# Pool stage of a four-layer graph network: matmul operands swapped, running maxima turned back, landing waits on GpSimd

## The reference, cut to what matters

```
def _graph_pool(out, adj):
    neg = jnp.finfo(out.dtype).min
    masked = jnp.where(adj_blk[:, :, None] != 0, out[None, :, :], neg)
    return jnp.max(masked, axis=1)          # for each block of rows
h = input @ weight
out = jnp.maximum(adj @ h + bias, 0.0)
return _graph_pool(out, adj)
```

## Time and profile before

| | us |
|---|---|
| median of three runs | 1762.82 (1762.29 to 1764.53) |
| profiled execution, own time | 1762.45 |
| its span, first to last instruction | 1760.7 |
| busy in the span: PE / DVE / ACT / POOL | 1564.3 / 1276.0 / 700.5 / 575.6 |
| mean granted TensorE clock | 0.965 of full |
| reduces of chunks (L1659), 256 | 172.8 |
| gathers of listed rows (L1302), 160 | 162.9 |
| selecting matmuls (L641), 3072 | 222.0 |

### The profile page before, as it was taken

The page is one execution under the profiler, slowest core; times in us unless marked ns, Lnnn a source line. Parts: engine busy times, 40 slices in busy tenths (PEclk is TensorE's granted clock), DMA queues, the critical chain, the costliest instruction groups (busy, mean ns, idle before and its releaser), DMA issues.

```text
span 1760.7 us, 37056 instructions
## 1 busy us (share of the span) xinstructions
PE 1564.3 (89%) x11433; PEld 1028.2 (58%) x11433; DVE 1276.0 (72%) x3508; ACT 700.5 (40%) x1113; POOL 575.6 (33%) x816
## 2 busy tenths in 40 slices
PE   3699999968888888999979999699999999889993
PEld 3467767647777777566646666578544444345552
DVE  5389999988999999455557666242599999944443
ACT  2334444425555555033332223466455555610000
POOL 2423233337777777011110001233000000047765
PEclk9999999988999999999999999899999999989997
DMA  4467777743433333222213223144100000024441
GB/s 156 174 250 262 289 271 288 286 151 90 122 113 101 113 100 116 82 96 95 93 34 125 83 88 114 55 132 125 37 1 6 6 12 6 6 91 154 152 140 48
DMA packets 97578, 205.11 MB, mean 116 GB/s; under 512 B 10912, under 2 KB 61728, under 8 KB 89328
## 3 DMA queue, kind: packets, MB, share of 16 engines
q1 hardware_dynamic: 73008, 172.58, 28.5%
q0 software_dynamic: 11840, 25.52, 5.2%
q10 hardware_dynamic: 12672, 6.29, 1.2%
HBM read 178.13 MB, written 26.21 MB: 116 GB/s over the span
## 4 chain that ended last, share of the span: by engine, by line
PE 45%; DVE 23%; issue 16%; POOL 9%; DMA 3%; ACT 2%; DVEq 1%; POOLq 1%; SPq 1%; ACTq 0%
PE bank L687 17%; PE bank L556 7%; PE bank L755 6%; DVE partsA L2063 6%; POOL gath L1385 5%; PE bank L822 4%; DVE gath L1659 3%; PE bank L641 3%; DVE cand L1526 2%; PE bank L561 2%; PE bank L541 2%; DMA gath<-last_features,idx_now 2%; PE bank L521 2%; POOL gath L1302 1%; PE bank L511 1%
## 5 line engine op out<-in xcount | busy, mean ns | idle before, releaser
L687 PE MATMUL bank<-partsB,panel 128*128 128x387 bf16 (+1 forms) x2048 | 354.5, 334 | 25.9 <-DVE agg L1460 12.1
L687 PEld LDWEIGHTS bank<-partsB,panel 128*128 128x128 fp8e4 x2048 | 202.7, 99 | 173.3 <-issue 27.1
L822 PE MATMUL bank<-wide,partsA 128*128 128x512 f32 x512 | 263.2, 596 | 6.3 <-ACT rows L1104 4.9
L641 PE MATMUL bank<-partsB,first 128*128 128x128 bf16 x3072 | 222.0, 221 | 35.6 <-DVE gath L1659 21.2
L1526 DVE MAX8 cand<-bank 128x8 f32<-128x128 f32 x1024 | 217.1, 279 | 42.1 <-POOL found L1213 21.7
L641 PEld LDWEIGHTS bank<-partsB,first 128*128 128x128 fp8e4 x3072 | 194.3, 98 | 80.7 <-issue 62.4
L556 PE MATMUL bank<-partsA,panel 128*128 128x387 bf16 x1024 | 218.1, 336 | 23.6 <-DVE cand L1526 14.3
L889 ACT ACTIVATE panel<-bank 128x1024 fp8e4<-128x1024 bf16 x128 | 130.7, 1023 | 175.9 <-PE bank L541 175.9
L1302 POOL DMA_INDIRECT gath<-pool_features,idx_now x160 | 162.9, 1018 | 55.3 <-issue 46.7
L1104 ACT COPY rows<-bank 128x512 f32<-128x512 f32 x256 | 133.3, 615 | 116.3 <-DVE partsA L2079 87.6
L1659 DVE TENSOR_REDUCE gath<-bank 128x128 f32<-128x512 f32 x256 | 172.8, 681 | 7.5 <-PE bank L641 7.1
(11 more groups left out here) (274 smaller groups left out, 2173.6 us busy)
## 6 DMA issues: line engine op xcount, KB each, us to landing
rows<-in_adj SPq DMA_DIRECT2D x64, 1024.0 KB, 7.2
panel<-adjT_panels SPq DMA_DIRECT2D x128, 512.0 KB
adjT_panels<-panel SPq DMA_DIRECT2D x32, 512.0 KB, 3.0
panel<-adjT_panels SPq DMA_DIRECT2D x64, 256.0 KB, 2.9
gath<-pool_features,idx_now POOLq DMA_INDIRECT x160
overflow_maxima<-wide POOLq DMA_DIRECT2D x1, 2048.0 KB, 19.1
pool_features<-gsc ACTq DMA_DIRECT2D x8, 256.0 KB, 2.3
rows<-overflow_maxima SPq DMA_DIRECT2D x8, 256.0 KB
```

Source lines behind the costliest of these rows:

```text
L641: i = pe.matmul(first_bank(n, peeled)[:, b * P:(b + 1) * P], first[:, q % 2, j, :], pparts[:, j, k * FE:k * FE + F], start=(k == 0), stop= ...
L687: i = pe.matmul(bank[q][:, 0:3 * w], panel[:, q, j, :], of_block if w < FE else parts_of[u][:, j, :], start=(j == 0), stop=(j == NT - 1))
L822: pe.matmul(o[:, :], zs[:, q % 2, :], zT[:, c * 512:(c + 1) * 512], start=True, stop=False)
```

## The change

TensorE. The operands of the selecting product are swapped: a 128 x 128 part of a block's features is stationary, and the selection codes of that block for *all four tiles* of the group (512 columns) stream past. So a step is now one block j of 32, with three matmuls of 512 columns, and its result has features as partitions and the group's 512 rows as columns. The triangular product is taken per block for four tiles (`tri_block`), from the panel laid out in pieces of four blocks (`piece`), six blocks ahead (`AHEAD`), through two banks. The selections lie in a ring of 16 slots.

VectorE. The maximum over blocks is now a running one of 128 x 512 in SBUF: blocks 0 and 1 are copied into two accumulators, blocks 2 to 31 are maxima of a bank with one of the accumulators in turn, and a last maximum joins the two. In the next group PE turns the result back by four transposes (`turn_firsts`), and `pool_floor` takes it from PSUM in a step of its own. The trees lose their first, widest step: only the five gathered rows remain, in three steps.

GpSimd. There are four slots for gathered rows and for indices, one for each tile of a group. `PAUSE` and `after_chunk` are gone. GpSimd waits till all five gathers of tile 0 have landed before those of tile 1, till tile 1's have landed before the overflow gathers, and till tile 2's have landed before those of tile 3. The scatter moves from the end of the group to behind tile 2's gathers.

SyncE loads eight pieces of 256 KB a group instead of four panels. ScalarE's copies for the next layer (`side_of`, `part0`) move into the group after, and the helper products use banks 6 and 7 of their own.

```diff
+        main = [gath[:, 0, 0:MAIN, :], gath[:, 1, 0:MAIN, :],
+                gath[:, 1, MAIN + FIRSTS + 1:2 * MAIN + FIRSTS + 1, :],
+                gath[:, 1, 2 * MAIN + FIRSTS + 1:3 * MAIN + FIRSTS + 1, :]]
+        running = gath[:, 0, MAIN:MAIN + FIRSTS, :].rearrange("p (a q) f -> p a (q f)", a=2)
-        tri_bank = [bank[2], bank[3], bank[6], bank[7]]
+        tri_bank = [bank[2], bank[3]]
...
             with sp.Fori(1, NG) as g:
-                for q in range(G):
-                    sp.wait_ge(s_tri, 8 * (g * G + q - G + 1))
-                    load_panel(g, q)
+                for c in range(NG):
+                    sp.wait_ge(s_tri, NT * (g - 1) + BPB * (c + 1))
+                    load_piece(g, c)
                 load_overflow(g - 1)
...
+            def tri_block(g, j):
+                if j % BPB == 0:
+                    pe.wait_ge(s_piece[j // BPB], 16 * (g + 1))
+                pe.wait_ge(s_first, NT * g + j + 1)
+                pe.matmul(tri_bank[j % 2][:, :], tri[:, :], piece[:, j // BPB, :, ts(j % BPB, P)],
                           start=True, stop=True).then_inc(s_tri, 1)
...
-                        for k in range(3):
-                            i = pe.matmul(first_bank(n, peeled)[:, b * P:(b + 1) * P], first[:, q % 2, j, :],
-                                          pparts[:, j, k * FE:k * FE + F], start=(k == 0), stop=(k == 2))
+            def select(g, j):
+                pe.wait_ge(s_first, NT * g + j + 3)
+                pe.wait_ge(s_fp_used, NT * g + j + 1)
+                for k in range(3):
+                    i = pe.matmul(pool_bank[j % 4][:, :], pparts[:, j, k * FE:k * FE + F], first_slot[:, j % SLOTS, :],
+                                  start=(k == 0), stop=(k == 2))
+                i.then_inc(s_fp, 1)
+            def turn_firsts(g):
+                pe.wait_ge(s_firsts_all, g + 1)
+                pe.wait_ge(s_side, g + 1)
+                for q in range(G):
+                    i = pe.transpose(psT[:, q * P:(q + 1) * P], firsts_all[:, q * P:(q + 1) * P], ident[:, :])
+                i.then_inc(s_turned, 1)
...
+            def rows_landed(g, q):
+                pool.wait_ge(s_gath[q], 16 * MAIN * (g + 1))
             def gathers(g, q):
                 t = g * G + q
                 pool.wait_ge(s_idx, t + 1)
                 pool.wait_ge(s_gath_used, t + 1)
+                if q in (1, 3):
+                    rows_landed(g, q - 1)
                 for k in range(MAIN):
-                    if k == PAUSE:
-                        after_chunk(t if q == 2 else t - 1, 1 if q == 2 else 6)
-                    pool.indirect_dma_start(gath[:, q % 2, k, :], None, feat_dram,
-                                            bass.IndirectOffsetOnAxis(idx_now[:, q % 2, k:k + 1], axis=0)
-                                            ).then_inc(s_gath[q % 2], 16)
+                    pool.indirect_dma_start(main[q][:, k, :], None, feat_dram,
+                                            bass.IndirectOffsetOnAxis(idx_now[:, q, k:k + 1], axis=0)
+                                            ).then_inc(s_gath[q], 16)
...
                     gathers(g, q)
                     if q == 1:
+                        rows_landed(g, q)
                         overflow_gathers(g)
-                store_overflow(g)
+                    if q == 2:
+                        store_overflow(g)
...
-                dve.tensor_reduce(gath[:, q % 2, MAIN + c, :],
-                                  first_bank(q * (NT // BPB) + c, peeled).rearrange("p (b f) -> p f b", b=BPB),
-                                  axis=AX, op=ALU.max).then_inc(s_fp_used, 1)
+            def take_block(g, j, first_group=False):
+                n = NT * g + j
+                if j < 2:
+                    if j == 0 and not first_group:
+                        dve.wait_ge(s_firsts_all, g)
+                    dve.wait_ge(s_fp, n + 1)
+                    dve.tensor_copy(running[:, j, :], pool_bank[j][:, :]).then_inc(s_fp_used, 1)
+                else:
+                    dve.wait_ge(s_fp_used, n + 3)
+                    dve.wait_ge(s_fp, n + 1)
+                    dve.tensor_tensor(running[:, j % 2, :], running[:, j % 2, :], pool_bank[j % 4][:, :], ALU.max
+                                      ).then_inc(s_fp_used, 1)
+                if j == NT - 1:
+                    dve.wait_ge(s_fp_used, n + 5)
+                    dve.tensor_tensor(firsts_all[:, :], running[:, 0, :], running[:, 1, :], ALU.max
+                                      ).then_inc(s_firsts_all, 1)
...
+                    dve.wait_ge(s_gath[q], 16 * MAIN * (g + 1))
+                    dve.tensor_tensor(slot[:, 0:2, :], slot[:, 0:2, :], slot[:, 2:4, :], ALU.max).then_inc(s_tree, 1)
...
+                for j in range(NT):
+                    take_block(g, j, peeled)
+                    if not (peeled or second):
+                        if j == 2:
+                            remainder(g - 2)
+                        if j == 25:
+                            part2(g - 2)
+                    if not peeled:
+                        if 3 <= j < 6:
+                            tree(before, G - 1, j - 3, (g, G - 1))
+                        if 6 <= j < 9:
+                            pool_floor(before, j - 6)
...
+                    for q, j0 in ((0, 11), (1, 17), (2, 26)):
+                        if j0 <= j < j0 + 3:
+                            tree(g, q, j - j0, None if last else (g + 1, q))
+                    if 21 <= j < 25:
+                        overflow_maxima(g, j - 21)
```

More of the change, by code:

```diff
@@ L36 @@
 MAIN = 5
-PAUSE = 3
+AHEAD = 6
+SLOTS = 16
 OVER = LIST - MAIN
@@ L603, in _ @@
                       ).then_inc(s_missing, 1)
+            for j in range(2, AHEAD):
+                tri_block(0, j)
             pe.wait_ge(s_flag, 1)
-            tri_chunk(0, 0, 2)
-            tri_chunk(0, 0, 3)
             pparts = parts_of[1]
[L610 to L626, removed]
@@ L663, in pool_turn @@
             def pool_turn(g, first_group, last):
[L664 to L675, removed]
+                for j in range(NT):
+                    if first_group:
+                        if j == 8:
+                            overflow_records()
+                    else:
+                        if j == 5:
+                            turn_firsts(g - 1)
+                        if j == 25:
+                            aux_transposes(1, g - 1)
+                        if j == 28:
+                            aux_products(1, g - 1)
+                    select(g, j)
+                    if j + AHEAD < NT:
+                        tri_block(g, j + AHEAD)
+                    elif not last:
+                        tri_block(g + 1, j + AHEAD - NT)
             pe.wait_ge(s_parts, 2 * NG)
@@ L912, in _, with first_block @@
             act.activation(DSTD[:, :], DEG[:, :], ACT.Sqrt).then_inc(s_sstd, 1)
[L914 to L919, removed]
-                                   tri_bank[c % 4][:, :], ACT.Relu, saturate=False).then_inc(s_first, 1)
+            def first_block(g, j, fresh=False):
+                act.wait_ge(s_tri, NT * g + j + 1)
+                if not (fresh and j < SLOTS):
+                    act.wait_ge(s_fp, NT * g + j - SLOTS + 1)
+                act.sem_inc(waited["act"], 1)
+                act.activation(first_slot[:, j % SLOTS, :], tri_bank[j % 2][:, :], ACT.Relu, saturate=False
+                               ).then_inc(s_first, 1)
             def after(u, s, g, more=None):
@@ L1757, in turn @@
                 before = 0 if second else g - 1
-                def at(q, c):
-                    take_firsts(g, q, c, peeled and q < 2, peeled)
-                at(0, 0)
-                if not (peeled or second):
-                    remainder(g - 2)
-                for c in range(1, 5):
-                    at(0, c)
-                    if not peeled:
-                        tree(before, G - 1, c - 1, (g, 1))
-                at(0, 5)
-                for c in range(6, 8):
-                    at(0, c)
-                    if not peeled:
-                        pool_floor(before, c - 6)
@@ L1774, in turn @@
-                if peeled:
-                    overflow_indices()
-                at(1, 0)
-                if not peeled:
-                    pool_post(before, 0)
-                for c in range(1, 5):
-                    at(1, c)
-                    tree(g, 0, c - 1, (g, 2))
-                if not (peeled or second):
-                    part2(g - 2)
-                for c in range(5, 8):
-                    at(1, c)
-                    if not peeled:
-                        pool_post(before, c - 4)
```

203 lines of the change are left out of this document (82 added, 121 removed).

## The result

The changed kernel takes 1787.05 us (median of four runs, 1786.95 to 1790.42) against 1763.09 for the kernel before on the same chip (four runs, 1762.29 to 1764.53): ratio 1.014 [1.0122, 1.0157]. The forecast was 1787.5. The profiled execution took 1786.95, 24.5 more than the 1762.45 of before.

What follows compares the result with a forecast made beforehand. GpSimd's gather issue, together with VectorE, was taken as the bound. Intervals 275.3, copies 7.0, slow gathers 9.6 and waits 36.0 made 327.9 us; with a shorter tail and 2 us for collisions, 1787.5, own range 1775 to 1798.

Steps and rivals of the forecast that it cites:

- the point on which all turned: GpSimd, 401 to 705 us: issues without a pause, about 5 us of 301 are waits; bounds the stage together with VectorE.
- slow gathers: GpSimd gathers held past 0.952 us by VectorE operations with two SBUF operands: 14.8 us before, 9.6 after.
- copies: GpSimd's one staging copy of overflow indices a group: 8 x 0.88, 7.0 us in the stage, before and after.
- landing waits: GpSimd, ahead of tile 1, overflow and tile 3 gathers: +2.05, +1.70, +0.75 us a group, 36.0 in all.
- 2 us for collisions: Added to the sum for gather landings that collide with the panel's 256 KB pieces: 2 us.
- The tail: From the last gather's start to the last group's normalised rows: 11.2 us instead of 14.9.
- TensorE and VectorE: Block of 2048 columns 0.875 us on TensorE, before 0.91; VectorE from 35.5 us busy a group to about 32.
- GpSimd does not bind: Rival for the gather stage: landing waits fall into idle time, groups run at 33.5 us, total 1729; chance 0.07.
- Waits at their lower bound: Rival on GpSimd's landing waits: 2.7 us a group, 21.6 in all, no holds, total 1764; chance 0.10 for 1764 to 1774.
- The dear case: Rival on GpSimd's gathers: block maxima hold them too (20 us), landings average 3.1 (16 us), total 1813; chance 0.13 above 1798.
- The Trainium skill's fit: Rival on gather landings: a 64 KB transfer takes 2.15 us, waits 7 us cheaper in all, total 1780; no chance given.

Runs made afterwards that it cites:

- experiments 1 to 5: Changed kernel with no landing waits (1747.71 us) or one of three (1765.23, 1762.60, 1756.06); kernel before with all three added, 1803.83 us.
- experiment 1: Changed kernel with its three landing waits taken out of GpSimd's list: 1747.71 us, ratio 0.9907; repeated, 1748.94 us, 0.9938.
- experiments 2 to 4: Changed kernel with only one landing wait kept: the first 1765.23 us, the second 1762.60, the third 1756.06.
- experiment 8: Changed kernel without landing waits, copy of the overflow indices moved ahead of tile 1's first gather: 1753.70 us, ratio 0.995.

## Why the prediction was right, point by point

**The bound.** That an engine with 74% busy share is the bound was the point on which all turned, and experiments 1 to 5 show it: taking waits away or adding them, in either order, moves the time by about what they add to GpSimd's stream. The stream of the changed kernel closes as that of before did. From the first gather's start (397.78) to the last's (731.23) are 220 intervals: 220 x 1.257 = 276.5; slow gathers 159.0 + 51.5 + 8.1 - 210.4 = 8.2; copies 2.7 + 6.5 - 8 x 0.30 = 6.8; landing waits 29.8 - 16 x 0.30 = 25.0 for first and third, 17.0 for the second. Together 333.5, measured 333.45.

**The terms.** Landing waits: 42.0, forecast 36.0, the one term that was clearly mis-sized. Per group the first and third took 3.13 (forecast 2.80), the second 2.13 (1.70). The working was with one landing of 2.45, and the median is 2.5, but five of the eight first waits are 2.56 to 3.14 long and four of the second 2.29 to 2.48, where the forecast's sizes are 2.3 and 1.7. The forecast's 2 us for collisions belonged here and should have been 6. Whether these landings do collide with the pieces' transfers no experiment tested. Slow gathers: 8.2, forecast 9.6, within what phase does. Copies: 6.8, forecast 7.0.

The stream is thus 333.45 where the forecast had 327.9 + 1.4 for the first interval = 329.3. The last gather still began at 731.23 against a forecast of 730.3, because in this profile the stream started at 397.78 and not at 400.96. That start varies from 397.5 to 403.7 over the kernels' profiles, though most of them are the same up to there. Part of the closeness of 1787.05 to 1787.5 is therefore luck: about 4 us too little in the stream, of which the 2 for collisions, added at the end, made good a half, and 3 too much in its start.

**The tail.** From the last gather to the normalised rows, answering to the earlier trace rows:

```profile
731.23 0.95 POOL L1282 DMA_INDIRECT gath<-pool_features,idx_now  x1 [0.30 <-issue]
733.73 0.43 DVE L1662 TENSOR_TENSOR gath<-gath 128x256 f32<-128x256 f32 x1 [3.03 <-DMA gath<-pool_features,idx_now]
741.18 1.11 DVE L1734 TENSOR_SCALAR hn<-xg,mv,rstd 128x128 f32<-128x128 f32 x4
```

Landed 2.50 after the start, normalised at 742.29: 11.1 us, forecast 11.2, before 14.9. From there to the end are 1786.95 - 742.29 = 1044.7, before 1762.45 - 718.49 = 1044.0.

**TensorE and VectorE.** A block of 2048 columns takes 0.865 (forecast 0.875, before 0.91): two of them from 561.07 to 562.80,

```profile
561.07 0.38 PE L585 MATMUL bank<-panel,tri 128*128 128x512 fp8e4 x1
561.29 0.81 PE L614 MATMUL bank<-first,partsB 128*128 128x512 fp8e4 x3
561.94 0.38 PE L585 MATMUL bank<-panel,tri 128*128 128x512 fp8e4 x1
562.15 0.81 PE L614 MATMUL bank<-first,partsB 128*128 128x512 fp8e4 x3
562.80 0.38 PE L585 MATMUL bank<-panel,tri 128*128 128x512 fp8e4 x1
```

Four matmuls of 512 columns in 0.865 are 0.216 each. The pace of 131 ns that the Trainium skill gives (TensorE: Matmul & The Clock Gate, Back-to-back issue gap) does not hold here. VectorE's 240.85 of 304 us are 33.0 in a group of 41.7, forecast about 32 in one of 41.0. It waits 49.1 / 8 = 6.1 us a group at the overflow step, forecast about 7.

**The rivals.** That GpSimd does not bind fell with experiment 1. Waits at their lower bound (2.7 a group) fell with experiments 2 to 4: 4.9. The dear case had the landings 16 us dearer than 2.45 each, where 6 were found, and let the block maxima hold gathers, which they don't. The Trainium skill's fit (DMA: Bandwidth & Descriptors, Anatomy of one DMA — SWDGE (gpsimd) path), 2.15 us for such a transfer, gives an estimate that would have made the waits 7 us cheaper; measured they are 6 us dearer than with 2.45.

## What to carry to other kernels

Before believing a busy share, add up the stream of an engine that issues: durations plus the fixed gap behind each instruction. If it closes with next to no wait, as here with 5 us of 301, the engine binds even at 74%, and relief elsewhere arrives only in the few us in which it waits for others. On such an engine a wait for one's own transfer costs its landing less the gap that stands there anyway, plus the late restart, here about 2 us each time; the one with a scatter in front of it cost about half of that or less. Where each tile has slots of its own, as here, the wait can be left to the engine that uses the rows; experiment 1 does that.

## What was not expected of the hardware

- The late restart belongs to the instruction that waits, not to the copy before it. A gather that waits for the staging copy of its own indices starts 0.81 behind it (627.39 above); a gather that follows the same copy and needs nothing of it starts 0.16 behind it (559.43 in experiment 8, and 0.16 or 0.17 in every group but the first).
- TensorE, idle for 8.88 us at the overflow step, came back at half its clock. The three matmuls of a block take 1.44 and 1.49 instead of 0.81, the level of 1.2 GHz instead of 2.4, and are at 0.81 again at 604.65; the granted clock is 0.53 from 598.2 to 604.6 and 1.00 from 604.7 to 620. Seven of the eight groups show it, behind 5.4 to 8.9 us of idle time; in the other TensorE was idle for 3.06 us and came back at 0.81 (636.67).

```profile
598.26 1.44 PE L614 MATMUL bank<-first,partsB 128*128 128x512 fp8e4 x3 [8.88 <-issue]
...
599.92 1.49 PE L614 MATMUL bank<-first,partsB 128*128 128x512 fp8e4 x3
...
604.65 0.81 PE L614 MATMUL bank<-first,partsB 128*128 128x512 fp8e4 x3
```

The mean granted clock of the stretch fell from 0.98 to 0.92. It cost next to nothing here: GpSimd, which sets the pace, waited for VectorE for only 0.9 us in the whole stage. On a kernel that TensorE binds, a wait elsewhere might be paid a second time in this way; no run here shows that.
